# Flamingo block on one core: silu and h moved ahead of the split of x in the expert slots, the rank read only where the expert changes, gathered rows added ahead of y at the end

## What is computed

```python
x = x + tanh(g_xattn) * mamba(ctx_1024, layernorm(x), ...)        # first stage
x = x + tanh(g_ffn)   * ffn(layernorm(x), ...)                    # second stage

def ffn(x):                                # E = 16 experts, K = 2, I = 352
    scores = softmax(x @ gate_w.T)
    topk_w, topk_idx = top_k(scores, 2)
    y  = sum over the two experts e of a token: topk_w * (silu(x @ Wg[e]) * (x @ Wu[e])) @ Wd[e]
    y += (silu(x @ Sg) * (x @ Su)) @ Sd    # shared expert, inner width 704
```

## Time and profile before

| | us |
|---|---|
| median of 3 runs (lowest to highest) | 1098.83 (1098.75 to 1099.41) |
| the profiled execution: its own time | 1099.88 |
| its span in the profile | 1098.3 |
| PE busy | 914.0 (83%) |
| DVE busy | 742.6 (68%) |
| ACT busy | 613.0 (56%) |
| POOL busy | 598.4 (54%) |

### The profile page before, as it was taken

The page is one execution under the profiler, slowest core; times in us unless marked ns, Lnnn a source line. Parts: engine busy times, 40 slices in busy tenths (PEclk is TensorE's granted clock), DMA queues, the critical chain, the costliest instruction groups (busy, mean ns, idle before and its releaser), DMA issues.

```text
span 1098.3 us, 22460 instructions
## 1 busy us (share of the span) xinstructions
PE 914.0 (83%) x5389; PEld 770.8 (70%) x5389; DVE 742.6 (68%) x1082; ACT 613.0 (56%) x1041; POOL 598.4 (54%) x522
## 2 busy tenths in 40 slices
PE   6579866988789876877999982999999999994787
PEld 3257555765567556756899971989999998883775
DVE  4779798877898798989776560644545555546456
ACT  4697997699778987796332220333444555543120
POOL 4457797778977796889211056022434444431344
PEclk9579998998999998899999995899999999995889
DMA  8105101340115103111311147245566656674456
GB/s 256 40 21 192 59 30 39 114 135 30 30 38 191 59 29 107 50 40 38 127 38 38 58 153 285 87 131 164 166 226 230 233 164 233 232 235 130 160 175 237
DMA packets 67447, 137.31 MB, mean 125 GB/s; under 512 B 9392, under 2 KB 15024, under 8 KB 67248
## 3 DMA queue, kind: packets, MB, share of 16 engines
q1 hardware_dynamic: 54736, 105.66, 29.1%
q0 software_dynamic: 8960, 29.37, 7.6%
q10 hardware_dynamic: 3680, 1.39, 0.6%
HBM read 163.53 MB, written 42.07 MB: 187 GB/s over the span
## 4 chain that ended last, share of the span: by engine, by line
PE 33%; SPq 5%; issue 5%; another core or an unknown queue 3%; ACT 2%; DVE 2%; POOL 2%; ACTq 1%; DMA 0%; POOLq 0%; DVEq 0%
PE psY L954 11%; PE psG L918 9%; PE psU L918 9%; PE psT L911 2%; PE psHT L932 2%; POOL weights L649 1%; SPq L440 1%; SPq L496 1%; SPq L495 1%; SPq L497 1%; SPq L434 1%; ACT weights L1233 1%; ACTq L1325 1%; DVE x_tok L1874 1%
## 5 line engine op out<-in xcount | busy, mean ns | idle before, releaser
L571 POOL TENSOR_TENSOR prod<-hst,cbc 128x512 f32<-128x512 f32 x256 | 335.1, 1334 | 89.4 <-PE y_ps L784 69.5
L1473 DVE TENSOR_TENSOR_SCAN hst<-dA,dbu_ps 128x512 f32<-128x512 f32 x256 | 304.6, 1209 | 66.8 <-PE dbu_ps L766 57.2
L766 PE MATMUL dbu_ps<-ident,dbuT 128*128 128x128 f32 x1024 | 170.3, 292 | 43.6 <-DVE hst L1473 22.2
L766 PEld LDWEIGHTS dbu_ps<-ident,dbuT 128*128 128x128 f32 x1024 | 124.6, 149 | 110.9 <-DVE hst L1473 53.5
L1280 ACT CAST hh<-psHT 128x384 fp32r<-128x384 f32 x79 | 37.7, 477 | 291.4 <-PE psHT L932 241.5
L1149 ACT ACTIVATE dA<-dts,Aneg 128x512 f32 (+1 forms) x256 | 169.0, 711 | 32.2 <-DVE hst L1473 31.7
L1160 ACT ACTIVATE dbuT<-duT,BT 128x512 f32 (+1 forms) x256 | 163.0, 708 | 0.0
L954 PE MATMUL psY<-weights,hh 128*128 (+3 forms) x420 | 137.0, 408 | 30.3 <-DVE hl L1670 24.5
L784 PE MATMUL y_ps<-ident,prod 128*128 128x128 f32 x1024 | 160.0, 283 | 2.6 <-POOL prod L571 2.6
L918 PE MATMUL psU<-weights,xh 128*128 (+2 forms) x560 | 143.9, 339 | 0.7 <-issue 0.7
L918 PE MATMUL psG<-weights,xh 128*128 (+1 forms) x560 | 137.8, 328 | 4.4 <-issue 2.3
(11 more groups left out here) (219 smaller groups left out, 1403.1 us busy)
## 6 DMA issues: line engine op xcount, KB each, us to landing
raw_gu<-in_L_ffn_w_gate_up_dram SPq DMA_DIRECT2D x100, 704.0 KB
raw_d<-in_L_ffn_w_down_dram SPq DMA_DIRECT2D x50, 512.0 KB
cbc<-c_rows SPq DMA_DIRECT2D x64, 256.0 KB, 3.2
slot_in<-ztile SPq DMA_DIRECT2D x3, 4096.0 KB, 13.6
gbuf<-slot_in SPq DMA_DIRECT2D x48, 256.0 KB, 3.2
slot_out<-yout POOLq DMA_DIRECT2D x48, 256.0 KB, 3.4
raw_d<-in_L_ffn_w_down_dram SPq DMA_DIRECT2D x50, 192.0 KB
xn_rows<-xin SPq DMA_DIRECT2D x16, 256.0 KB, 2.0
```

What stands on the lines that cost most here:

```text
L571: pool.tensor_tensor(prod[:, prod_slot(n, j), :], hst[:, slot_of(n, j), :], cbc[:, n % 2, :], ALU.mult).then_inc(prod_ready, 1)
L766: last = tr(dbu_ps[j % 2][:, t * P:(t + 1) * P], dbuT[:, n % 2, t, j * P:(j + 1) * P], ident[:])
L1473: V.tensor_tensor_scan(hst[:, slot_of(n, j), :], dA[:, slot_of(n, j), :], dbu_ps[j % 2][:], 0.0, ALU.mult, ALU.add).then_inc(scanned, 1)
```

## The change

On ScalarE silu of G(q) now stands ahead of the copy `xh`. On VectorE h(q) stands ahead of `xl`, so in slots with work in `before_h` that work, too, comes ahead of `xl`. In the routed slots VectorE reads `chg_i` after the result, and `rank_i` only inside the branch for a change. At the end the gathered rows of tiles are added earlier: one tile's two additions go ahead of the next to last `hl`, one tile's into the last slot ahead of its result, and the last tile's ahead of the last product, so that the last instruction of VectorE is that product's addition. SP then stores the last two tiles by the count of results (`y_read`), the others by the count of additions (`f_added`, which takes the place of `f_done`). The diff, less the renamed semaphore in two places:

```diff
@@ SP, the stores at the end
+            QE = Q1 + NT - NB1
+            def store_out(t):
+                sp.dma_start(out_t[:, bass.ds(t, 1), :], x_tok[:, bass.ds(t, 1), :]).then_inc(out_stored, 16)
-            with sp.Fori(0, NB1) as m:
+            with sp.Fori(0, NB1 - 2) as m:
                 for k in range(2):
-                    t = m + k * NB1
-                    sp.wait_ge(f_done, m * 2 + k + 1)
-                    sp.dma_start(out_t[:, bass.ds(t, 1), :], x_tok[:, bass.ds(t, 1), :]).then_inc(out_stored, 16)
+                    sp.wait_ge(f_added, m * 2 + k + 1)
+                    store_out(m + k * NB1)
+            sp.wait_ge(f_added, 2 * NB1 - 3)
+            store_out(NB1 - 2)
+            sp.wait_ge(f_added, 2 * NB1 - 1)
+            store_out(NB1 - 1)
+            sp.wait_ge(y_read, QE - 2 + 1 + 2)
+            store_out(NT - 2)
+            sp.wait_ge(y_read, QE - 1 + 1 + 2)
+            store_out(NT - 1)
@@ ScalarE, slot
-                if not last_slot and not late:
+                act.wait_ge(g_done, q + 1)
+                nc.scalar.activation(sg[:, k, :], psG[k][:, 0:INTER], ACT.Silu).then_inc(sg_ready, 1)
+                if not last_slot:
                     x_hi(q + 1, 1 - k)
                 if load is not None:
                     act.dma_start(xin[:, 1 - k, :], xn_rows[bass.ds(load * P, P), :]).then_inc(xin_ready[1 - k], 16)
-                act.wait_ge(g_done, q + 1)
-                nc.scalar.activation(sg[:, k, :], psG[k][:, 0:INTER], ACT.Silu).then_inc(sg_ready, 1)
-                if late:
-                    x_hi(q + 1, 1 - k)
@@ VectorE, slot
                 if not first:
                     h_lo(q - 1, 1 - k)
-                if not last_slot and not late:
-                    x_lo(q + 1, 1 - k)
...
                 V.tensor_tensor(hbuf[:, k, 0:INTER], sg[:, k, :], psU[k][:, 0:INTER], ALU.mult
                                 ).then_inc(h_ready, 1)
+                if not last_slot and not late:
+                    x_lo(q + 1, 1 - k)
                 if before_result is not None:
@@ VectorE, routed_slot
-                slot(r + Q0, k, kind, r - 1 if kind == "routed" else NB1 - 1, before_result=read_tables)
-                rank = table["rank"]
-                buf = (rank + 1) % 2
-                with dve.If(table["chg"]):
+                slot(r + Q0, k, kind, r - 1 if kind == "routed" else NB1 - 1)
+                chg = dve.value_load(chg_i[0:1, bass.ds(r, 1)], min_val=0, max_val=1)
+                with dve.If(chg):
+                    rank = dve.value_load(rank_i[0:1, bass.ds(r, 1)], min_val=0, max_val=NE)
+                    buf = (rank + 1) % 2
                     split_gu_lo(rank + 3, lambda w: w[:, bass.ds(buf, 1)].rearrange("p a k c -> p (a k) c"),
                                 chunks=KH - 1)
@@ VectorE, the end
+            def last_of_pair6():
+                add_routed(2 * NB1 - 3, 1, NT - 2)
+                dve.wait_ge(f_added, 2 * NB1 - 2)
             slot(QE - 2, 0, "shared", NT - 3)
-            finish_pair(NB1 - 3, QE - 3, 1)
-            slot(QE - 1, 1, "shared", NT - 2, last_slot=True)
+            add_pair(NB1 - 3, QE - 3, 1)
+            add_routed(2 * NB1 - 4, 0, NB1 - 2)
+            slot(QE - 1, 1, "shared", NT - 2, last_slot=True, before_result=last_of_pair6)
             h_lo(QE - 1, 1)
-            finish_pair(NB1 - 2, QE - 2, 0)
-            finish((2 * NB1 - 2, 2), NB1 - 1)
+            add_routed(2 * NB1 - 2, 2, NB1 - 1)
+            add_routed(2 * NB1 - 1, 3, NT - 1)
+            dve.wait_ge(f_added, 2 * NB1)
             result_to(QE - 1, 1, "shared", NT - 1)
-            dve.wait_ge(y_read, QE + 2)
-            finish((2 * NB1 - 1, 3), NT - 1)
```

More of the change, by code:

```diff
@@ L306, in flamingo_block @@
         f_first = sem("f_first")
-        f_done = sem("f_done")
+        f_added = sem("f_added")
         out_stored = sem("out_stored")
@@ L668, in _ @@
                 if i >= 4:
-                    pool.wait_ge(f_done, i - 3)
+                    pool.wait_ge(f_added, i - 3)
                 for c in range(2):
@@ L1867, in _, with add_routed @@
             Q1 = Q0 + SLOTS
-            def finish(i, t):
-                i, k = i
-                dve.wait_ge(gathered[k], 32 * ((i >> 2) + 1))
+            def add_routed(i, k4, t):
+                dve.wait_ge(gathered[k4], 32 * ((i >> 2) + 1))
                 for c in range(2):
-                    ins = V.scalar_tensor_tensor(token_tile(t), gathered_rows(k, c),
+                    ins = V.scalar_tensor_tensor(token_tile(t), gathered_rows(k4, c),
                                                  wts[:, c, bass.ds(t, 1)], token_tile(t), ALU.mult, ALU.add)
@@ L1878, in finish, with add_pair @@
                         dve.wait_ge(f_first, i + 1)
-                ins.then_inc(f_done, 1)
-            def finish_pair(n, q, parity):
-                finish((n * 2, 2 * parity), n)
+                ins.then_inc(f_added, 1)
+            def add_pair(n, q, parity):
+                add_routed(n * 2, 2 * parity, n)
                 dve.wait_ge(y_read, q + 1 + 2)
-                finish((n * 2 + 1, 2 * parity + 1), n + NB1)
+                add_routed(n * 2 + 1, 2 * parity + 1, n + NB1)
             slot(Q1, 0, "routed", SLOTS - 1)
             slot(Q1 + 1, 1, "shared", NB1)
-            finish_pair(0, Q1, 0)
+            add_pair(0, Q1, 0)
             with dve.Fori(1, (NT - NB1) // 2 - 1) as m:
@@ L1892, in _ @@
                     slot(m * 2 + k + Q1, k, "shared", m * 2 + k + NB1 - 1)
-                    finish_pair(m * 2 + k - 1, m * 2 + k - 1 + Q1, 1 - k)
+                    add_pair(m * 2 + k - 1, m * 2 + k - 1 + Q1, 1 - k)
             QE = Q1 + NT - NB1
+            def last_of_pair6():
+                add_routed(2 * NB1 - 3, 1, NT - 2)
+                dve.wait_ge(f_added, 2 * NB1 - 2)
             slot(QE - 2, 0, "shared", NT - 3)
-            finish_pair(NB1 - 3, QE - 3, 1)
-            slot(QE - 1, 1, "shared", NT - 2, last_slot=True)
+            add_pair(NB1 - 3, QE - 3, 1)
+            add_routed(2 * NB1 - 4, 0, NB1 - 2)
+            slot(QE - 1, 1, "shared", NT - 2, last_slot=True, before_result=last_of_pair6)
             h_lo(QE - 1, 1)
-            finish_pair(NB1 - 2, QE - 2, 0)
-            finish((2 * NB1 - 2, 2), NB1 - 1)
+            add_routed(2 * NB1 - 2, 2, NB1 - 1)
+            add_routed(2 * NB1 - 1, 3, NT - 1)
+            dve.wait_ge(f_added, 2 * NB1)
             result_to(QE - 1, 1, "shared", NT - 1)
-            dve.wait_ge(y_read, QE + 2)
-            finish((2 * NB1 - 1, 3), NT - 1)
 _INS = ['x', 'ctx_1024', 'g_xattn', 'g_ffn', 'L0_xattn_in_proj_w', 'L0_xattn_conv_w', 'L0_xattn_conv_b',
```

## The result

| | before | after |
|---|---|---|
| median of 4 runs | 1098.79 us | **1152.05 us** |
| range | 1098.30 to 1099.41 | 1150.33 to 1153.84 |
| ratio, 95% interval | | **1.0493** [1.0468, 1.0518] |
| span of the profiled execution | 1098.3 us | 1148.7 us (its own time 1150.33) |

Slower, as forecast, but by 53 us instead of 7, and far outside the range of 1101.5 to 1110.5.

A forecast was written before the change was run, and what follows sets the result against it. Bound: TensorE's chain, with `hl` right behind VectorE's weight subtractions at a change. Terms 7.1 - 0.3 + 0.9 + 0.6 - 1.3 = +7.0 us on 1098.83 gave 1105.8 us; 8-in-10 range 1101.5 to 1110.5.

The forecast's parts named there:

- What bounds the kernel: Change of expert: `hl` stands right behind VectorE's weight subtractions, no slack left; delaying them delays TensorE by as much.
- The table reads: Routed slots: reads behind the result's copy leave VectorE idle 1.2 us at each of 16 changes: +7.1 us.
- the sign that I gave: Weight subtractions, routed stage: about 19 us idle before them, ended by the sequencer ("issue"), no longer by ScalarE.
- The low end: Range's lower bound, 1101.5 us: reads cost +4.2, only six changes paying 0.7 each.
- the two terms on the unused slots: Slots not used, last routed result: +0.9 and +0.6 us; off the path in the DMA rival (-1.5).
- The sequencer stands still at an unmet wait: VectorE's sequencer stops at an instruction whose semaphore has not come, so reads cannot run while the result waits.
- the first rival: Table reads run ahead of the result, by the skill's wait queue: 1098.7 us, no change; chance 0.07.
- Used slots, h ahead of `xl`: Used slots: `xl` ends 1.2 us after U, TensorE needs it 2.09 after; +0.
- Scatter: Around the scatter: positions start 0.6 us earlier, late `xl` costs +0.3; sum -0.3, bounds -0.6 and +0.7.
- Unused slots: Slots not used: silu between `hh` and `xh` costs 0.1 us in each of 9: +0.9, bounds 0 and 1.4.
- Last result and end: Last routed result's copy behind `xl`: +0.6 us; additions moved earlier at the end: -1.3, bounds -0.5 and -1.8.
- Slower still: Rival: waits for no engine grow, among the scatters or gathers: +3 to +6 us, 1109 to 1112; chance 0.09.

The follow-up runs named there:

- e11: Kernel before, with small idle VectorE work between the second and third weight subtraction of a change, in two sizes for even and odd slots: ratio 1.0046.
- e4: Whole change, but GpSimd's first subtraction of a change waits until VectorE's three are done; reads stay behind the result: ratio 1.0111.
- e1: Whole change, but with both table reads put back ahead of the result: ratio 1.0020.
- e3: Whole change, but the flag `chg_i` is read ahead of the result and only the rank behind the branch: ratio 1.0024.
- e9: e4 plus two more reads of the rank behind the branch, making TensorE's pause long again: ratio 1.0481.
- e5: Whole change, but down begins with its six products of `hh` and waits for `hl` only ahead of the last three: ratio 1.0137.
- b0: Kernel before, unchanged, profiled on the third of the four other chips; one run, U 259.6, S 58.4, N 42.6 us.
- e2: Kernel before, with only the table reads moved: both behind the result, the rank behind the branch: ratio 1.0491.
- e6: Kernel before, with the new order alone (h ahead of `xl`, silu ahead of `xh`); reads and end as before: ratio 1.0024.
- e8: Kernel before, with down's six `hh` products first, waiting for `hl` only ahead of the last three, and the new end too: ratio 0.9971.
- e7: Kernel before, with the new end alone (routed rows added ahead of the last results): ratio 1.0000.

## Why the prediction was wrong

*What bounds the kernel* held: "whatever delays them delays TensorE by as much" is true of `hl`, and e11 shows it to 0.4 us of delay (U +5.3 for 4.3).

*The table reads*: the step that failed is the sum "VectorE is idle for 1.2 us at each of 16 changes, 19.2 in all, against 11.9 now: +7.1". The idle time was right (1.24; 19.6 in all; its releaser is still put down to ScalarE, against the sign that I gave). What failed is that every later step was taken to keep its length, so that the cost of what stands behind the delay stood in the sum at nothing. Two steps did not keep it:
- the third subtraction, 2.40 instead of 0.89 us, 16 x 1.5 = 24 us. e4 takes it away by moving GpSimd, e1 and e3 by moving VectorE.
- TensorE's clock behind the pause, 12 x 1.43 = 17 us in down and some in G. e9 has it without the first, and e5 has the first without it.

With 31.6 us of new pauses (24 of them the held third, 7.6 the delay: my 7.1) and 17.2 of slow downs, the 51.0 of stretch U are told but for 2.2. The delay by itself, in e4, is rather more than my term: VectorE is idle there for 21.1 us ahead of the subtractions against 11.3 in b0, and TensorE loses 9.3. Both high and low end of the range were lengths of reads; no bound was set for what stands behind them. (The low end, 1101.5, also needs the two terms on the unused slots at nothing; the reads at their low end alone give 1102.9.) A row that would have warned stands in the trace before, and I passed over it: GpSimd's first subtraction took 2.03 us, with the end of VectorE's third in it, though its next ones of 512 columns took 1.28 (704 columns would be 1.76 by proportion, and e4 shows 1.71). It was being held already. The Trainium skill (SBUF — State Buffer, SBUF: two separate sides) states the rule that I did not weigh: VectorE and GpSimd share one pair of ports, an instruction of VectorE with two inputs in SBUF and one of GpSimd that reads SBUF exclude each other, and whichever starts first keeps the pair for its whole length. The trace agrees in both directions, 2.41 = 1.66 to the end of GpSimd's first + 0.75, and 2.42 for GpSimd in e11; and `hl`, which has one input in PSUM, takes 0.55 beside GpSimd as without it.

*The sequencer stands still at an unmet wait*: right, so the first rival is out. The reads ran behind the copy's start at 749.45, and even the register step ahead of the copy ran at 749.31, when down was over (749.27). Had the reads run ahead of the copy, e2 would have cost nothing.

*Used slots, h ahead of `xl`*: right, U 259.8 in e6 against 259.6.

*Scatter*: -0.7 where I had -0.3. It hung on a condition, "inside that wait", and that is what decides its sign: on the first chip ScalarE is stopped for 31.7 us and the late `xl` is hidden; on the others it is not stopped, and the same order costs 2.1 us.

*Unused slots*: not shown, +0.9 forecast. 42.4 against 41.4 looked like it, but among kernels with the old order N runs from 41.6 (e2) to 43.2 (e8); profiles scatter by more than the term.

*Last result and end*: -0.7 forecast, -1.3 in the profile of E, and 1.0000 in the timed pair of e7. Not told apart from nothing.

*The rivals*: none of the four was this one. "Slower still" had a chance of 0.09 and a price of 3 to 6 us, in another place.

## What to carry to other kernels

Where two engines take turns on a resource, read the distance between their starts, not only the durations: up to that distance a delay costs itself, and past it the rest of the other's instruction as well. Here 0.46 us of room was all there was at most changes. A sum over a moved wait must ask of each instruction behind it whether it meets a new neighbour, and of TensorE what a pause does to its clock. And the products that need the operand that comes last should stand last: three of nine need `hl`, and putting them last is worth 0.5% by itself and takes most of the price off a late `hl` (1.0137 instead of 1.0493).

## What the runs showed that I had not expected

- A pause of TensorE of 1.9 to 2.5 us in otherwise dense work lowers the granted clock at most places (12 of 16, 11 of 16 and 13 of 16 in three kernels) and not at all of them; pauses of 0.6 to 1.2 us did so nowhere in e4 and e5. The Trainium skill (TensorE: Matmul & The Clock Gate, HAM oscillation) tells of a kernel in which TensorE waits for a DMA between groups of products and starts each group cold. These rows agree in kind, for shorter waits, and not for every one of them.
- A subtraction of VectorE that meets GpSimd's waits for the end of the whole instruction. It is not slowed in proportion: the two lengths found are 0.88 to 0.89 and 2.39 to 2.44 us, with nothing between. It was held in 16 of 16, 16 of 16 and 14 of 16 changes of three kernels, and which of the two it is turns on 0.07 us of starting time.
- ScalarE's stop of 31.7 us during the scatter, which the profile puts down to no engine, is there in both kernels on the first chip and in no profile on the four others, where stretch S takes 58 to 62 us instead of 87 to 88. What it is was not found. The 29.5 us of S are most of the 33 us by which the kernel before is faster on the others.
